# Adaptive-norm feed-forward kernel: a small product in single passes, and both ends rearranged

## What is computed

```python
xq = quantize(x, thresholds, deltas, zero_points)      # 8 groups, 64 levels
mid = xq @ A.T ; logits = xq @ router_w.T              # 4 experts of rank 16
gates = softmax(top2(logits))
y = x + 4 * sum_e gates[e] * (mid[e] @ B[e].T)
h = y @ W.T + 0.5 * (y @ lora_A[label[b]]) @ lora_B_w.T
out = y + h @ K + bias + (h @ A_eff[b].T) @ B_eff[b].T + (h @ A_s.T) @ B_s.T
```

## Time and profile before

| | us |
|---|---|
| median of three runs | 442.15 |
| lowest and highest | 441.48, 442.58 |
| the profiled execution, whole | 441.27 |
| its span, first to last instruction | 439.5 |
| TensorE busy | 426.8 (97%) |
| VectorE busy | 384.3 (87%) |
| ScalarE busy | 363.7 (83%) |
| GpSimd busy | 59.8 (14%) |
| granted TensorE clock | 0.999 of full |

### The profile page before, as it was taken

The page is one execution under the profiler, slowest core; times in us unless marked ns, Lnnn a source line. Parts: engine busy times, 40 slices in busy tenths (PEclk is TensorE's granted clock), DMA queues, the critical chain, the costliest instruction groups (busy, mean ns, idle before and its releaser), DMA issues.

```text
span 439.5 us, 5658 instructions
## 1 busy us (share of the span) xinstructions
PE 426.8 (97%) x2136; PEld 341.4 (78%) x2136; DVE 384.3 (87%) x394; ACT 363.7 (83%) x314; POOL 59.8 (14%) x55
## 2 busy tenths in 40 slices
PE   8999999999999989979999999999999999999995
PEld 8877677888878878758777877787778778877873
DVE  1697979989999999999999899999999999999300
ACT  1599999938988888999989989999999998995002
POOL 0000004000040000130412213222130210330000
PEclk9999999999999999999999999999999999999999
DMA  7999539960479945370781862938870970283024
GB/s 265 352 309 408 177 85 292 197 160 0 119 244 268 274 107 195 69 183 1 172 152 23 186 175 45 210 68 182 179 172 20 191 134 1 52 153 47 9 40 95
DMA packets 40173, 66.09 MB, mean 150 GB/s; under 512 B 26994, under 2 KB 27250, under 8 KB 37874
## 3 DMA queue, kind: packets, MB, share of 16 engines
q0 software_dynamic: 8368, 38.28, 37.6%
q1 hardware_dynamic: 31778, 27.45, 21.9%
HBM read 55.23 MB, written 18.87 MB: 169 GB/s over the span
## 4 chain that ended last, share of the span: by engine, by line
PE 36%; DVE 30%; ACT 12%; issue 10%; DMA 9%; SPq 2%; ACTq 0%; DVEq 0%
DVE val L760 14%; DMA wst<-w_in 9%; PE bank L1217 8%; PE bank L1219 7%; PE bank L1218 7%; DVE val L742 6%; ACT val L484 5%; ACT level L471 4%; PE bank L1191 4%; DVE inside L751 3%; PE bank L1061 3%; PE bank L1030 2%; DVE p_lo L925 1%; DVE kp_lo L808 1%; ACT tst L617 1%
## 5 line engine op out<-in xcount | busy, mean ns | idle before, releaser
L760 DVE COPY_PREDICATED val<-inside,val 128x2048 f32<-128x2048 uint8 x56 | 143.0, 2553 | 0.3
L484 ACT ACTIVATE val<-level,shift,small 128x2048 f32<-128x2048 int16 x64 | 133.7, 2091 | 1.9 <-PE bank L1061 1.9
L471 ACT ACTIVATE level<-xq,inv 128x2048 int16<-128x2048 f32 x64 | 127.7, 1997 | 0.6
L1217 PE MATMUL bank<-p_hi,x_hi 128*128 128x512 f32 x256 | 107.4, 420 | 0.0
L1219 PE MATMUL bank<-p_hi,x_lo 128*128 128x512 f32 x256 | 100.1, 391 | 0.0
L1218 PE MATMUL bank<-p_lo,x_hi 128*128 128x512 f32 x256 | 99.9, 390 | 0.0
L742 DVE TENSOR_SCALAR val<-val,width,unshift 128x2048 f32<-128x2048 f32 x64 | 86.4, 1350 | 3.9 <-ACT val L484 3.8
L751 DVE TENSOR_SCALAR inside<-absx,thr 128x2048 uint8<-128x2048 f32 x56 | 72.2, 1290 | 0.0
L1217 PEld LDWEIGHTS bank<-p_hi,x_hi 128*128 128x128 f32 x256 | 48.1, 188 | 14.2 <-issue 5.1
L1218 PEld LDWEIGHTS bank<-p_lo,x_hi 128*128 128x128 f32 x256 | 48.1, 188 | 11.8 <-issue 3.1
L1219 PEld LDWEIGHTS bank<-p_hi,x_lo 128*128 128x128 f32 x256 | 48.1, 188 | 10.5
(11 more groups left out here) (118 smaller groups left out, 512.7 us busy)
## 6 DMA issues: line engine op xcount, KB each, us to landing
out_t<-bias_in POOLq DMA_DIRECT2D x8, 1024.0 KB, 16.9
out_t<-ost POOLq DMA_DIRECT2D x15, 512.0 KB, 7.6
wst<-w_in SPq DMA_DIRECT2D x14, 512.0 KB, 8.7
xq<-xt_in POOLq DMA_DIRECT2D x7, 1024.0 KB, 8.2
x_hi<-xt_in POOLq DMA_DIRECT2D x7, 1024.0 KB, 6.7
x_lo<-xt_in POOLq DMA_DIRECT2D x14, 512.0 KB, 6.0
la<-la_in SPq DMA_DIRECT2D x4, 512.0 KB, 5.6
kst<-k_in SPq DMA_DIRECT2D x4, 512.0 KB, 13.4
```

The lines of the kernel that those rows point to most:

```text
L471: nc.scalar.activation(level[:, g % 2], xq[:, c % 2], ACT.Copy, scale=inv[:, group(g)]).then_inc(levels_made, 1)
L484: nc.scalar.activation(val[:, turn(c, g)], level[:, g % 2], ACT.Relu, bias=shift[:, group(g)], scale=par[:, 1, group(g)]).then_inc(raised, 1)
L760: nc.vector.copy_predicated(val[:, acc(c)], inside[:, g % 2], val[:, turn(c, g)]).then_inc(merged, 1)
L1217: mm(o, x_hi[b % 3][:, k, at], p_hi[:, h, k], start=k == 0 and n < OWN, stop=False)
```

## The change

- Warm-up products: 5 in place of 7.
- The loads of small and of the labels move from SP's queue to the head of POOL's.
- betp lies in bet's own place; ScalarE copies half as much.
- bu_begin: 8 products of 128 columns, betp (rest | rounded) by ubp (rounded | rest), in float32r, into columns 256 to 383 of zbank, all 128 rows. ScalarE's bu_out copies one part (rest x rounded), and VectorE's new bu_add adds two others to it. bu_begin(c) now waits for ub_lo(c), z_begin(c) and z_end(c) wait for the sum.
- For batch 0, ub_hi and ub_lo stand ahead of the last p_out, bu_begin(0) between the two halves of bp's product and bu_out(0) ahead of bp_lo_out. For the others ub_hi stands at slot j = 0 in place of 3, ub_lo at 1 in place of 3, x_neg and x_rest at 0 and 1 in place of 0 and 2, the sum at 4.
- The quantizer's groups end two slots later (LAST); LAGS and the first entries of TAKEN differ; ZEND is 4 at least; for the last batch CLOSE is one slot behind ZEND.
- In the last batch the closing product may come first in a tile rather than last, for tiles n with 2n >= CLOSE[b] ("early").

```diff
-WARM, WARMUPS = 256, 7
+WARM, WARMUPS = 256, 5
-    betp, _ = place("betp", [P, KT, 2 * ER], F32R, ost_at)
+    betp, _ = place("betp", [P, KT, 2 * ER], F32R, bet_at)
-    LAGS = [(3, 3, 6, 7, 8, 9), (3, 3, 3, 4, 4, 6), (2, 4, 4, 6, 7, 9), (2, 3, 3, 4, 5, 6), (3, 6, 6, 7, 8, 9), (2, 3, 4, 5, 5, 7), (1, 2, 2, 4, 5, 6), (2, 2, 2, 3, 4, 5)]
-    TAKEN = [1, 0, 1, 2, 2, 1, 1, 1, 1, 1, 1, 1, 1, 1, 1, 1, 1, 2]
+    LAGS = [(3, 3, 7, 7, 8, 9), (3, 3, 3, 4, 4, 6), (2, 4, 4, 7, 8, 9), (2, 3, 3, 5, 5, 6), (3, 7, 8, 9, 10, 11), (2, 4, 4, 5, 5, 6), (1, 2, 2, 5, 6, 7), (3, 3, 3, 3, 4, 5)]
+    TAKEN = [0, 1, 1, 2, 2, 1, 1, 1, 1, 1, 1, 1, 1, 1, 1, 1, 1, 2]
-    LAST = STEPS + BATCH * KT - 9
+    LAST = STEPS + BATCH * KT - 7
-    XAT, UHAT, ULAT, BUAT, ZAT, ZLAT = (0, 2), 3, 3, 3, 5, 7
+    XAT, UHAT, ULAT, BUAT, ZAT, ZLAT = (0, 1), 0, 1, 3, 5, 7
-    ZEND = [max(b * KT, OUT_AT[b] - STEPS, 3) for b in range(BATCH)]
-    CLOSE = [max(b * KT + 1, ZEND[b] + HOLD) for b in range(BATCH)]
+    ZEND = [max(b * KT, OUT_AT[b] - STEPS, 4) for b in range(BATCH)]
+    CLOSE = [max(b * KT + 1, ZEND[b] + (HOLD if b + 1 < BATCH else 1)) for b in range(BATCH)]
...
+            pool.dma_start(small, a["small"]).then_inc(small_in, 16)
+            pool.dma_start(itok_sb, itok).then_inc(itok_in, 16)
             for c in range(1, BATCH):
...
-            sp.dma_start(small, a["small"]).then_inc(small_in, 16)
-            sp.dma_start(itok_sb, itok).then_inc(itok_in, 16)
...
                 if c:
                     act.wait_ge(z_read, c)
+                    act.wait_ge(bufull, c)
...
-                nc.scalar.activation(bu[2 * R:P, c % 2], zbank[ER:2 * ER, TOK:TOK + 2 * R], ACT.Copy).then_inc(bu_made, 1)
+                nc.scalar.activation(bu[2 * R:P, c % 2], zbank[0:ER, TOK:TOK + 2 * R], ACT.Copy).then_inc(bu_made, 1)
...
-                    nc.scalar.activation(betp, bet, ACT.Copy).then_inc(bet_hi_made, 1)
+                    nc.scalar.activation(betp[:, :, ER:2 * ER], bet[:, :, ER:2 * ER], ACT.Copy).then_inc(bet_hi_made, 1)
...
+            def bu_add(c):
+                dve.wait_ge(bu_made, c + 1)
+                row = bu[2 * R:P, c % 2]
+                nc.vector.tensor_tensor(row, zbank[ER:2 * ER, TOK:TOK + 2 * R], row, ALU.add).then_inc(bu_step, 1)
+                dve.wait_ge(bu_step, c + 1)
+                nc.vector.tensor_tensor(row, zbank[ER:2 * ER, TOK + 2 * R:TOK + 4 * R], row, ALU.add).then_inc(bu_summed, 1)
+
+            bu_add(0)
...
+                    if b + 1 < BATCH and j == BUAT + 1:
+                        bu_add(b + 1)
...
-                t = c % 2
-                pe.wait_ge(ub_in[t], 32 * (c // 2 + 1))
-                pe.wait_ge(bet_in, 16)
+                pe.wait_ge(ub_lo_made, c + 1)
                 if c:
                     pe.wait_ge(z_copied, 2 * c)
-                    pe.wait_ge(bu_made, c)
...
-                    last = mm(zbank[ER:2 * ER, TOK:TOK + 2 * R], bet[:, k, ER:2 * ER], ub[:, t, k], start=k == 0, stop=k == KT - 1)
+                    last = mm(zbank[:, TOK:TOK + 4 * R], betp[:, k], ubp[:, k].rearrange("p h c -> p (h c)"), start=k == 0, stop=k == KT - 1)
...
-                pe.wait_ge(bu_made, c + 1)
+                pe.wait_ge(bu_summed, c + 1)
...
                 o, at = cols[n % CRING], slice(t * P, (t + 1) * P)
+                early = b == BATCH - 1 and 2 * n >= CLOSE[b]
+                if part == 0 and early and 2 * n > CLOSE[b]:
+                    mm(o, zt[:, b % ZSLOTS, at], tb[:, b % 2, h * HALF:(h + 1) * HALF], start=True, stop=False)
```

More of the change, by code:

```diff
@@ L207, in build @@
     mg_zeroed = sem("mg_zeroed")
-    bufull, bu_made = sem("bufull"), sem("bu_made")
+    bufull, bu_made, bu_step, bu_summed = sem("bufull"), sem("bu_made"), sem("bu_step"), sem("bu_summed")
     zfull, zt_made = sem("zfull"), sem("zt_made")
@@ L696, in _ @@
                     gate_exp(EXP[n])
+            ub_hi(0)
             p_out(STEPS - 1)
@@ L701, in _ @@
                 x_part(p)
-            ub_hi(0)
+            bu_out(0)
             for c, g in GROUPS[STEPS + 1]:
@@ L705, in _ @@
             bp_lo_out()
-            bu_out(0)
             eyes()
@@ L943, in _ @@
                 ranks(n)
+            ub_lo(0)
             p_out(STEPS - 1)
@@ L946, in _ @@
                 x_part(p)
-            ub_lo(0)
+            def bu_add(c):
[5 more added lines that the diff above has]
+            bu_add(0)
             dve.wait_ge(bias_hi_made, 1)
@@ L1186, in _ @@
                 last.then_inc(bpfull, 1)
-            bu_begin(0)
+                if h == 0:
+                    bu_begin(0)
             def close(n):
@@ L1214, in _ @@
                         pe.wait_ge(bias_made, 1)
-                    mm(o, ones, bias[:, h * HALF:(h + 1) * HALF], start=True, stop=False)
+                    mm(o, ones, bias[:, h * HALF:(h + 1) * HALF], start=not (early and 2 * n > CLOSE[b]), stop=False)
                 for k in range(part * KT // 2, (part + 1) * KT // 2):
-                    mm(o, x_hi[b % 3][:, k, at], p_hi[:, h, k], start=k == 0 and n < OWN, stop=False)
+                    mm(o, x_hi[b % 3][:, k, at], p_hi[:, h, k], start=k == 0 and n < OWN and not (early and 2 * n > CLOSE[b]), stop=False)
                     mm(o, x_hi[b % 3][:, k, at], p_lo[:, h, k], start=False, stop=False)
-                    last = mm(o, x_lo[:, s, k, at], p_hi[:, h, k], start=False, stop=False)
-                if j == KT - 1:
+                    last = mm(o, x_lo[:, s, k, at], p_hi[:, h, k], start=False, stop=early and k == KT - 1)
+                if early and part:
+                    last.then_inc(ofull, 1)
+                elif j == KT - 1:
                     last.then_inc(x_done, 1)
@@ L1236, in _ @@
                         close(m)
-                elif part and q > CLOSE[b]:
+                    if early and part == 0:
+                        mm(o, zt[:, b % ZSLOTS, at], tb[:, b % 2, h * HALF:(h + 1) * HALF], start=False, stop=False)
+                elif part and q > CLOSE[b] and not early:
                     close(n)
```

## The result

The changed kernel takes 453.88 us (median of 4 executions, 453.75 to 456.01) where the kernel before takes 442.37 in the same session (441.48 to 444.73): a ratio of 1.0263, 95% interval 1.0213 to 1.0313. It is 2.6% slower. The forecast was 441.4 us, in a range of 439.2 to 443.2. The profiled execution took 453.96 us with a span of 452.2; the forecast for that span was 438.8, so 13.4 us have to be found.

A forecast was written before the change was run, and what follows sets the result against it. Bound by TensorE's products, VectorE's groups close second. TensorE's end 434.98 + 1.8 - 3.35 - 0.6 + 0.1 - 0.8 = 432.1 us, + 6.65 = 438.8 span, 0.7 below before; 442.15 - 0.7 = 441.4 us, range 439.2 to 443.2.

The forecast's parts named there:

- The kernel's two lines: Two queues of nearly equal length side by side: products on TensorE (97% busy), the quantizer's groups on VectorE (87%).
- the wait of bu(1): Batch 1's bu product: TensorE waits 4.9 us near 187 us for VectorE's ub_lo(1), in place of 0.7 + 2.4.
- VectorE does not become the end: Rejects the sixth rival, VectorE's last merge late through the adds: 445.4 us at 1.2 us more a batch, chance 0.08.
- the adds: VectorE's two dependent adds over 64x64: 0.5 us a batch (0.4 to 0.8), 4.0 us in all, no wait taken.
- a tie at gated_turn(4): Batch 4's gate stands a group further back on VectorE, its turn two slots back: 0.1 us taken, 0 to 1.1.
- signs of being wrong: VectorE idle ahead of the bu adds, a wait near 187 us under 3 us, or over 1 us at turns or mids.
- Part 1: The start: la's loads issued earlier through moved small loads, two warm-ups fewer; 0.8 us gained, bounds 0 and 1.3.
- part 4: New waits around batch 1: junction 0.2 us later, TensorE waiting at bu(1), mid(2) starting 1.8 us later than before.
- The fifth rival: The start gives nothing, a late gmix or the DMA queue taking it back: 442.2 us, chance 0.10.
- Part 2: The new bu product takes 0.45 us, 0.65 saved each; 3.35 us saved in batches 2 to 7.
- the fourth rival: Short bu products cost more: 0.09 us each, 443.1 us, chance 0.12; or 0.12 each, 445.4 us, chance 0.04.
- Part 5: The tail: "early" never acts, POOL's last store comes late; span ends 6.65 us behind TensorE against 4.5, 2.15 lost.

The follow-up runs named there:

- a_warm10: The changed kernel with ten warm-ups in place of five, small still on POOL's queue; 447.87 us, one execution.
- a_small_sp: The changed kernel with the loads of small and the labels back on SP's queue, still five warm-ups; 455.25 us, one execution.
- b_warm5: The kernel before with five warm-ups in place of seven, nothing else; 443.82 us, one execution.
- The filler: a_start_old with 36 products without use on TensorE ahead of the waiting bu(1); 446.5 us, ratio 1.0069.
- a_hold0: a_start_old with the last batch's closing one slot earlier, which lets "early" act; 447.52 us, one execution.
- a_start_old: The changed kernel with the whole old start, small and labels on SP's queue and seven warm-ups; 448.9 us, ratio 1.0134.
- a_old_bu_hold0: a_start_old with the new bu product, its adds and waits taken out, and the last batch's closing one slot earlier; 441.55 us, ratio 0.9988.
- a_comb: a_start_old with ub_lo(1) at slot 0, z_begin(1) one slot later and the last batch's closing one slot earlier; 449.21 us, ratio 1.016.
- b_best: b_close6 with ub_hi and ub_lo at slots 0 and 1, the last batch closing one slot earlier and "early" acting; 439.24 us, ratio 0.9942.
- b_start: The kernel before with only the start of the change, small and labels on POOL's queue and five warm-ups; 448.81 us, one execution.
- a_ub_first: a_start_old with VectorE making ub_lo(1) at slot 0 in place of slot 1; 446.82 us, one execution.
- b_close6: The kernel before with the first batch closing one slot later and mid(2) one slot later; 441.82 us, ratio 0.9993.

## Why the prediction was wrong

**What it had right.** The kernel's two lines; the wait of bu(1) and what releases it (4.4 us for 4.9), with TensorE and VectorE both there some 7 us later than forecast, by the start; that VectorE does not become the end; the adds (0.46 us for 0.5); that "early" never acts and that the late POOL store then sets the end; the place of a tie at gated_turn(4) (0.9 us, in its bounds of 0 to 1.1). One of its signs of being wrong did show: VectorE was idle ahead of the adds, twice, 1.3 us in all waiting for bu_out's copy, where it took no wait. The traces give no sign that this decided anything.

**Part 1, the start, is the step that failed.** It took 0.8 us of gain and put the bounds at 0 and 1.3, with "a late gmix costs only what goes beyond that". This is true of the lateness (a_warm10) and false of the kernel: fewer warm-ups leave TensorE not yet at full clock (a_small_sp, 1.2 GHz up to 24.5 us), or the late load leaves it idle behind them and the clock falls again (13.7 us at 1.2 GHz in the changed kernel). Measured: 6.75 us later at the token half, where part 1 has 0.8 earlier and the junction of part 4 gives 0.2 of that back. The fifth rival ("the start gives nothing") looked the same way and stopped at zero. The error was to treat the warm-ups as time that can be saved, when in the traces they are what the clock hangs on. Even as time they were misread: 0.73 us each is the mean over two paces, and the last two take 0.9 us together, so "up to 1.5 us" was 0.5 in b_warm5. The two paces stand in the trace of the kernel before, and I never asked what the warm-ups are for. The share of the start by the timed kernels is 1.0263 less 1.0134, 1.3%.

**Part 4 was right in the wait and short in its price.** Behind the wait the clock is at 1.2 GHz until 203.8 us; the prediction put this at nothing without a reason. From bu(1) to mid(2) the prediction counts 13.9 us, measured are 17.1. The products between 198.2 and 203.8 at half speed are about 2.8 of these 3.2 us, the dearer bu product the rest. The filler gave 1.4 us of the like back in a run where the dip was milder.

**Part 2 read the right row with the wrong divisor.** 0.84 us is nearer the other end (1.0, the single ident product) than the 0.45 taken. I had divided gated_turn's 0.45 us by eight passes; but the trace gives it 4 records, each with a weight load of its own (x4 in the earlier trace rows), and the bu product 8 (x8). By the record it is 0.11 us in the one and 0.105 in the other, so 8 of them are 0.9 us by the same row. Saved for each of batches 2 to 6 is 0.3 us (1.17 less 0.84) and not 0.65, and batches 1 and 7 lose 0.3. That is the fourth rival, between its cheap form (0.09 us each, to which I gave 0.12) and its dear one (0.12 each, 0.04). The saving in batches 2 to 7 is then 1.35 us in place of 3.35; with the 0.8 us by which the wait at gated_turn(4) exceeds the 0.1 taken, this accounts for the 2.5 us in the third line of the table, with 0.3 to spare. By the figure of the Trainium skill, "TensorE: Matmul & The Clock Gate", section "Back-to-back issue gap" (81 ns for a pair), it would have been 0.65 us; measured are 105 ns for each, so this stream does not reach it.

**Part 5 was right in kind and 1.15 us short.** The store is issued 0.3 us ahead of TensorE's end and not 0.5. From its issue to the span's end it takes 8.1 us; in the kernel before it takes 7.7 (431.80 to 439.5), and I had counted 7.15: the landing at 6.5 us, which is 6.9 now, and 0.65 behind it, which is 1.2 in both traces. Both SP stores of 256 KB now leave within 1.1 us of it, and the second takes 6.0 us to landing, 3.3 before. The landings go with this company: in a_hold0, where SP's second store leaves 3.9 us after POOL's, they are 6.3 us and 3.1, in a_start_old, where it leaves 1.1 us after, 6.9 and 5.9.

**The range** was too narrow because its slower side held only dearer instructions. No case had a TensorE that runs slower in products that the change does not touch.

Left open: whether small lands late for POOL's queue or for the la loads that are now ahead of it; where a_start_old loses the part of its time before the token half that no clock entry explains; why the clock falls behind a wait for w_lo of 1.8 to 2.0 us near 158 us in a_start_old, a_hold0 and a_old_bu_hold0 and not behind one of 1.9 in a_comb or 2.1 in b_best; and how much more b_best would gain with x_rest a slot earlier, which was not tried.

## What to carry to other kernels

Before a warm-up is cut or a load is moved off the path, ask what TensorE's clock will be when the first real products come: 1.3 to 1.5 us of idle time cost 5 to 6 us here (b_start against b_warm5, the changed kernel against a_warm10), while a load 4 us late behind a busy TensorE cost nothing. A cheaper product that has to wait for a second engine's queue is priced by the wait and by the slow stretch behind it, and moving the wait (a_ub_first, a_comb, b_close6) found the next one on the same engine here. Where the last store takes 6 to 7 us to land, closing its tile a slot earlier gained some 2.7 us here though TensorE ended no sooner.

## What the runs showed that was not expected

- A load of 20 KB on POOL's queue took 5.3 us to land beside 2 MB of la on SP's queue, against 1.7 us at the head of SP's.
- The moment at which the clock rises at the start differs between runs whose warm-ups begin alike: 4.7 us in b_warm5, 5.2 in the kernel before, 6.1 in a_warm10, and 24.5 in a_small_sp, where TensorE had been busy without a gap since 1.2 us.
- In a_small_sp the view of the clock said 1.00 while 64 products took 13.9 us instead of 7.25, because the trace's clock entries begin only with the rise at 24.5 us. The same holds for the first 5 us of the other traces: the pace of the products is the better witness there.
- The same 2.4 us wait for zt(0) left the clock at full in the profiled execution of the kernel before and dropped it in b_warm5 (0.66 from 198 to 202 us). That this is a part of why the kernel before spreads from 440.6 us upwards is likely and not shown.
